# The start of each message-passing step of a graph layer: order of the first loads, place of one wait, and who clears the aggregation buffer

## The chip, the cores and the metric

The kernel runs on one core of a Trainium2 chip. The metric is the device time of one execution in microseconds (us), as the median of several runs. Engines are named as in the profile: PE (TensorE, with PEld for its weight loads), DVE (VectorE), ACT (ScalarE), POOL (GpSimd), SP (SyncE, which here only issues DMAs).

## The reference, cut to what matters

A graph layer over 3125 nodes with 256 channels and 50000 edges of three types. Three parts add up: gated graph convolution (below), a polynomial attention ("mix"), and an expert feed-forward part ("ffn").

```
def _gated_graph_conv(x, src, dst, emask, W, wih, whh, bih, bhh):
    h = x
    for i in range(STEPS):                    # 3 steps
        m = h @ W[i]
        msg = m[src] * emask[:, None]
        agg = segment_sum(msg, dst, num_segments=N)
        h = _gru_cell(agg, h, wih, whh, bih, bhh)
    return h
...
for t in range(T):                            # 3 edge types
    emask = (edge_type == t).astype(h.dtype)
    h_msg = h_msg + _gated_graph_conv(h, src, dst, emask, conv_w[t], gru_wih[t], ...)
```

## The kernel before

The program is a row of stages with a barrier between them: edge tables, normalisation, mix, the graph convolution (`gnn`, about 646 to 2457 us of the profiled execution), ffn. The change is inside `gnn`.

`gnn` does three steps (s = 0, 1, 2). The product with W[i] is moved behind the sum over edges, so a step first gathers rows of h and sums them by destination, and then multiplies by the product of the two weight matrices. A step has these parts:

- POOL gathers rows of h from a table in HBM (`tables[s]`: `xn_rows` in step 0, `h_rows` after), 128 edges at a time, by indirect DMA. Two gathers make a batch. One "pre" batch (line 1408) is followed by 195 main batches (line 1415), which fill a ring of 12 slots. So POOL issues 392 gathers in a step, one after another. The pre gather waits for an index tile (`pre_idx`) that DVE copies at line 1237; in steps 1 and 2 POOL waits before that for all stores of `h_rows`, which SP issues at line 1463.
- DVE makes a one-hot matrix for each batch (line 1238 for pre, 1260 for main), PE multiplies it with the gathered rows (line 1086, 8 matmuls a batch), and DVE adds the result to the right columns of `agg` (line 1245 for pre, 1257 for main). `agg` holds 6 x 3184 fp32 numbers in each partition and must be zero when the first batch is added. ACT clears it by eight activations (`act_clear`, line 1198), one for each group of nodes (NG = 8 groups of 224, 448 x 6 and 224 nodes); each adds one to the semaphore `cleared`.
- `pe_lead`: PE makes the weight products of type 0 (line 1114, 16 matmuls, which ACT copies to `g_wc`), the pre batch, the products of type 1, main batches 0 to 2, the products of type 2, and batches 3 to 8. The raw weights lie in buffers that hold node columns later: type 0 in `hn`, type 1 in `hT[1]`, type 2 in `hn` again. So the load of type 2 waits for the products of type 0.
- Then come 48 units (8 groups of nodes x 3 types x 2 halves of the channels) with the gates of the GRU cell (line 1163 on PE). Between their matmuls stand the other batches, at places written out beforehand by a planner (`PLAN`); before the first unit of group g, 24, 55, 87, 120, 152, 185, 195 batches must be in for g = 1 to 7. After the last gather lands, some 90 us of units are left in a step.

Every engine runs its instructions in the order in which they are written, so a wait holds up all that stands behind it. SP issues the loads of `gnn` in this order in step 0: node columns of group 0 (`load_states(0)`, three DMAs of 224 KB), the biases `bi` and `bh`, the three recurrent weights `wh` (768 KB each), then the raw weights (`load_weights`: 768 + 256 KB for each type).

In `dve_pre` the wait for `cleared` stands ahead of the copy of the indices:

```
step(e.tensor_copy(pre_at[:, :], bases[:, :]))
e.wait_ge(S["cleared"], NG * (s + 1))
...
e.tensor_copy(pre_idx[:, :], idx[...]).then_inc(V[s]["idx"], 1)
```

Of the kernel before, what the change touches and what calls it, by code (L numbers as in the profile page):

```python
# [10 lines left out]
ALU = mybir.AluOpType  # L11
# [5 lines left out]
P = 128  # L17
# [936 lines left out]
def halves_before(n):  # L954

    return sum(halves(i) for i in range(n))
# [36 lines left out]
def gnn(nc, A, tables, cols, idx0, idx1, keys, bases, main_at, shift, tab, iota_keys, ident, acc_rows, xf):  # L993

    with ExitStack() as ctx:
# [232 lines left out]
        def dve_pre(e, s):  # L1228
            rounds, number = pre_rounds(e)
            step = counted(e, V[s]["set"], 0)  # L1230
            step(e.memset(pre_shift[:, :], 0.0))
            step(e.tensor_copy(pre_at[:, :], bases[:, :]))
            e.wait_ge(S["cleared"], NG * (s + 1))
            idx = idx1 if s else idx0
            with e.Fori(0, rounds) as r:
                with e.Fori(0, number) as b:
                    e.tensor_copy(pre_idx[:, :], idx[:, bass.ds(b * BATCH + FIRST, BATCH)]).then_inc(V[s]["idx"], 1)  # L1237
                    e.scalar_tensor_tensor(out=onehot[:, 0, :, :], in0=iota_keys[:, :].unsqueeze(1).to_broadcast([P, BATCH, NKEY]), scalar=pre_shift[:, 0:1],
                                           in1=keys[:, bass.ds(b * BATCH, BATCH)].unsqueeze(2).to_broadcast([P, BATCH, NKEY]), op0=ALU.add, op1=ALU.is_equal).then_inc(V[s]["onehot"], 1)
                    e.tensor_copy(pre_now[:, :], pre_at[0:1, bass.ds(b, 1)]).then_inc(V[s]["now"], 1)  # L1240
                    e.wait_ge(V[s]["now"], r * NB + b + 1)
                    e.sem_inc(V[s]["seen"], 1)
                    o = e.value_load(pre_now[0:1, 0:1], min_val=0, max_val=NP)
                    e.wait_ge(V[s]["batch"], r * NB + b + 1)
                    e.tensor_tensor(agg[:, :, bass.ds(o, DT)], agg[:, :, bass.ds(o, DT)], pagg[0][:, :, :], ALU.add).then_inc(V[s]["added"], 1)
                    e.wait_ge(V[s]["added"], r * NB + b + 1)
                step = counted(e, V[s]["set"], r * 2 + 2)
                step(e.tensor_scalar(pre_shift[:, :], pre_shift[:, :], float(DT), None, ALU.add))
                step(e.tensor_scalar(pre_at[:, :], pre_at[:, :], DT, NP, ALU.add, ALU.min))  # L1249
            e.sem_inc(V[s]["done"], 1)  # L1250
# [144 lines left out]
        with nc.Block() as block:  # L1395
# [22 lines left out]
            def _(e):  # L1418
                def load_states(G):
# [6 lines left out]
                    for t in range(TYPES):  # L1426
# [1 line left out]
                        if s:  # L1428
                            e.wait_ge(col_store[t], 16 * ((s - 1) * NG + g + 1))
                        e.dma_start(hT[G % 2][:, t, :, 0:width(g)], src[:, :, node_at(g):node_at(g) + width(g)]).then_inc(h_in[G % 2], 16)  # L1430
                def load_weights(s):
                    for t in range(TYPES):
                        wi, wm = raw(t)
                        if s and t == 0:
                            for i in range(TYPES):
                                e.wait_ge(col_store[i], 16 * NG * s)
                            e.wait_ge(S["turn"], halves_before(TYPES * NG * s))
                        if s and t == 1:
                            e.wait_ge(S["pz"], s * UNITS)
                            e.wait_ge(S["d"], s * UNITS)  # L1440
                        if t == 2:
                            e.wait_ge(S["product"], 4 * TYPES * s + 4)
                        e.dma_start(wi, A["wihT"][t].rearrange("(k p) n -> p k n", p=P)).then_inc(w_type[t], 16)
                        e.dma_start(wm, A["convT"][t, s].rearrange("(k p) n -> p k n", p=P)).then_inc(w_type[t], 16)

                def load_base(g):
                    e.dma_start(base_of(g)[:, :, 0:width(g)], cols[0][:, :, node_at(g):node_at(g) + width(g)]).then_inc(base_in[g % 2], 16)
                load_states(0)
                e.dma_start(bi[:, :, :], A["bihT"]).then_inc(S["b_in"], 16)
                e.dma_start(bh[:, :, :], A["bhhT"]).then_inc(S["b_in"], 16)  # L1450
                for t in range(TYPES):
                    e.dma_start(wh[:, t, :, :], A["whhT"][t].rearrange("(k p) n -> p k n", p=P)).then_inc(S["w_in"], 16)
                load_weights(0)
                for G in range((STEPS - 1) * NG):
                    s, g = G // NG, G % NG
                    a, W = node_at(g), width(g)
                    load_states(G + 1)
                    for t in range(TYPES):
                        n = TYPES * G + t
                        e.wait_ge(S["hnew"], G * NU + KC * (t + 1))  # L1460
                        e.dma_start(cols[s + 1][t][:, :, a:a + W], hn[:, t, :, 0:W]).then_inc(col_store[t], 16)
                        e.wait_ge(S["rows_lo"], halves_before(n + 1))
                        e.dma_start(tables[s + 1][a + t * NP:a + t * NP + W, :].rearrange("(a p) c -> p a c", p=PT), rows16[n % 2][:, 0:W // PT, :]).then_inc(row_store[n % 2], 16)
                    if g == NG - 1:
                        load_weights(s + 1)
                s = STEPS - 1
                for v in range(UNITS + 6):
                    g = v // NU
# [36 lines left out]
            @block.scalar  # L1505
            def _(e):
                e.wait_ge(S["zero"], 1)
                for g in range(NG):
                    act_clear(e, 0, g)
                e.wait_ge(S["set"], 1)  # L1510
                for s in range(STEPS):
                    act_products(e, s)
                    for v in range(UNITS):
                        act_unit(e, s, v)
                        act_turn(e, s, v)
                        if last(s):
                            act_spreads(e, v)
                        if not last(s) and UNITS - NU <= v < UNITS - 1:
                            act_clear(e, s + 1, v - (UNITS - NU))
                    act_turn(e, s, UNITS)  # L1520
                    if last(s):
                        for v in range(UNITS, UNITS + 6):
                            act_spreads(e, v)
                    if not last(s):
                        for g in range(NU - 1, NG):
                            act_clear(e, s + 1, g)

            @block.vector
            def _(e):
                e.memset(zero[:, :], 0.0).then_inc(S["zero"], 1)  # L1530
                e.wait_ge(S["b_in"], 32)
                e.tensor_tensor(brz[:, :, :], bi[:, :, :], bh[:, :, :], ALU.add).then_inc(S["set"], 1)
                step = counted(e, S["rank"], 0)
                for s in range(STEPS):
                    dve_pre(e, s)
                    dve_batches(e, s, 0)
                    for v in range(UNITS + (6 if last(s) else 2)):
                        if v < UNITS:
# [390 lines left out]
```

## Time and profile before

| | |
|---|---|
| median of 3 runs | 3043.88 us (3043.86 to 3047.2) |
| the profiled execution, its own time | 3049.32 us |
| its span in the trace | 3047.6 us |
| PE busy | 2602.3 us (85%) |
| POOL busy | 1291.3 us (42%) |
| DVE busy | 1592.3 us (52%) |
| ACT busy | 651.8 us (21%) |
| mean granted TensorE clock | 0.927 of full speed |

Busy time is the sum of an engine's instructions, averaged over stages with different limits. Times in the trace count from the start of the span.

### The profile page before, as it was taken

The page shows a single profiled execution, that of the slowest core. Times are in us where ns is not written, and L with a number is a line of the kernel's source. Part 1 is how long each engine was busy: PE and PEld are TensorE (multiplying, and loading weights), DVE is VectorE, ACT ScalarE, POOL GpSimd, SP SyncE. Part 2 cuts the span into 40 slices and gives each one's busy share as a digit, 9 for nine tenths or more (in the row PEclk, how much of TensorE's full clock was granted, in tenths as well). Part 3 has the DMA queues.
Part 4 walks back from the last instruction along what each step waited for, and adds up shares of the span by engine and source line. Part 5 has one row for each costly group of instructions (what it writes and reads, how often), then busy time and mean ns, then how long its engine had stood idle before and what let it go on. Part 6 is the DMA issues. An engine that isn't in the chain of part 4 may idle for free. (4 is left out here: it accounts for less than half of the span.)

```text
span 3047.6 us, 39832 instructions
## 1 busy us (share of the span) xinstructions
PE 2602.3 (85%) x13041; PEld 1681.5 (55%) x13041; DVE 1592.3 (52%) x3093; ACT 651.8 (21%) x1191; POOL 1291.3 (42%) x1342
## 2 busy tenths in 40 slices
PE   1589899968999999889999997988988948999990
PEld 1343445536555555665555566555444647888880
DVE  4469887725555554465655544667777742000003
ACT  0321100031111112411111133122212312333320
POOL 0000000027777772377777705777777001111126
PEclk6699899989999999899999998999999957999995
DMA  1330076544454552544555425444444160222113
GB/s 50 104 106 1 1 266 231 203 138 133 140 157 145 157 157 83 155 144 133 152 159 156 148 90 158 133 130 141 140 139 134 34 197 24 64 92 90 62 50 115
DMA packets 211512, 374.19 MB, mean 123 GB/s; under 512 B 28898, under 2 KB 163459, under 8 KB 211206
## 3 DMA queue, kind: packets, MB, share of 16 engines
q1 hardware_dynamic: 149318, 203.45, 20.4%
q0 software_dynamic: 62016, 168.51, 19.3%
q8 instruction: 94, 1.54, 0.2%
q14 instruction: 84, 0.69, 0.1%
HBM read 299.54 MB, written 72.31 MB: 122 GB/s over the span
## 5 line engine op out<-in xcount | busy, mean ns | idle before, releaser
L1415 POOL DMA_INDIRECT g_ring<-h_rows,idx x780 | 771.6, 989 | 237.8 <-issue 207.0
L1086 PEld LDWEIGHTS g_pagg<-g_onehot,g_ring 128*128 128x128 f16 x4704 | 324.9, 98 | 404.7 <-issue 267.5
L1086 PE MATMUL g_pagg<-g_onehot,g_ring 128*128 128x144 f16 x4704 | 393.8, 228 | 139.7 <-DMA g_ring<-h_rows,idx 89.8
L1415 POOL DMA_INDIRECT g_ring<-xn_rows,idx x390 | 383.1, 982 | 118.9 <-issue 105.8
L1257 DVE TENSOR_TENSOR g_agg<-g_agg,g_pagg 128x288 f32 x585 | 265.7, 454 | 250.7 <-PE g_pagg L1086 207.8
L1260 DVE SCALAR_TENSOR_TENSOR g_onehot<-iota_keys,shift,keys 128x288 f16<-128x288 f16 x585 | 299.4, 513 | 1.0 <-DVE g_pre_at L1249 1.0
L1889 DVE TENSOR_TENSOR f_ys<-f_bank,f_b 128x256 f32<-128x256 f32 x58 | 24.6, 425 | 411.6 <-PE f_bank L1841 411.6
L1349 DVE SCALAR_TENSOR_TENSOR g_t<-g_ph,g_bh,g_rT 128x448 f32<-128x448 f32 (+1 forms) x144 | 90.0, 625 | 267.6 <-PE g_ph L1163 253.5
L1163 PE MATMUL g_pi<-g_agg,g_wc 128*128 128x448 f32 (+1 forms) x576 | 226.6, 517 | 0.0
L1163 PE MATMUL g_pr<-g_hT,g_wh 128*128 128x448 f32 (+1 forms) x576 | 223.9, 512 | 0.0
L1163 PE MATMUL g_pr<-g_agg,g_wc 128*128 128x448 f32 (+1 forms) x576 | 220.6, 506 | 0.0
L1163 PE MATMUL g_pz<-g_hT,g_wh 128*128 128x448 f32 (+1 forms) x576 | 219.7, 504 | 0.0
L1211 ACT ACTIVATE g_nT<-g_t,g_bi 128x448 f32<-128x448 f32 (+1 forms) x144 | 89.5, 622 | 607.8 <-DVE g_t L1356 607.8
L1163 PE MATMUL g_ph<-g_hT,g_wh 128*128 128x448 f32 (+1 forms) x576 | 218.8, 503 | 0.0
L1163 PE MATMUL g_pz<-g_agg,g_wc 128*128 128x448 f32 (+1 forms) x576 | 218.3, 501 | 0.0
L1841 PE MATMUL f_bank<-f_w,f_hid 128*128 128x256 f32 x928 | 207.9, 382 | 6.0 <-ACT f_hid L1864 6.0
L1833 PE MATMUL f_bank<-f_slotsT,f_w 128*128 x928 | 207.1, 382 | 1.0 <-ACT f_slotsT L1857 1.0
L1408 POOL DMA_INDIRECT g_ring<-xn_rows,g_pre_idx x2 | 2.1, 1044 | 472.1 <-DVE g_pre_idx L1237 471.8
L1841 PEld LDWEIGHTS f_bank<-f_w,f_hid 128*128 128x128 f32 x928 | 173.9, 190 | 35.2 <-issue 12.7
L1833 PEld LDWEIGHTS f_bank<-f_slotsT,f_w 128*128 128x128 f32 x928 | 177.7, 192 | 25.9 <-issue 1.4
L1777 POOL COPY f_now<-f_idx 128x2 int32 x30 | 5.5, 183 | 403.2 <-PE f_bank L1631 321.4
L1207 ACT ACTIVATE g_rT<-g_pr,g_brz 128x448 f32<-128x448 f32 (+1 forms) x144 | 84.5, 587 | 417.4 <-PE g_pr L1163 417.2
(345 smaller groups left out, 3465.5 us busy)
## 6 DMA issues: line engine op xcount, KB each, us to landing
ma_R<-q_cols SPq DMA_DIRECT2D x27, 896.0 KB, 9.8
f_w<-in_L_ffn_W SPq DMA_DIRECT2D x16, 1024.0 KB, 7.5
h_cols<-g_hn SPq DMA_DIRECT2D x36, 448.0 KB, 4.4
h_rows<-g_rows SPq DMA_DIRECT2D x36, 448.0 KB, 3.5
g_hT<-h_cols SPq DMA_DIRECT2D x36, 448.0 KB, 5.9
mix_R<-q_cols SPq DMA_DIRECT2D x15, 896.0 KB, 10.0
g_ring<-h_rows,idx POOLq DMA_INDIRECT x780
ma_R<-q_cols SPq DMA_DIRECT2D x9, 1120.0 KB, 5.6
```

The costliest lines, as they stand in the source:

```text
L1086: mm = e.matmul(pg[:, k * TYPES:(k + 1) * TYPES, :].rearrange("p t d -> p (t d)"), ring[:, slab, c, o:o + P], hot[:, c, :], start=(c == 0 ...
L1163: mm = e.matmul(p[:, 0:W], w, x, start=(first and k == 0), stop=(final and k == KC - 1), skip_group_check=True)
L1207: e.activation(rT[:, 0:W], pr[:, 0:W], ACT.Sigmoid, bias=brz[:, t, m:m + 1]).then_inc(S["r"], 1)
L1211: e.activation(nT[:, 0:W], t1[:, 0:W], ACT.Tanh, bias=bi[:, t, 4 + m:5 + m]).then_inc(S["n"], 1)
L1257: e.tensor_tensor(agg[:, :, bass.ds(o, DT)], agg[:, :, bass.ds(o, DT)], pagg[b % BANKS][:, :, :], ALU.add).then_inc(S["added"], 1)
L1260: e.scalar_tensor_tensor(out=onehot[:, b % 4, :, :], in0=iota_keys[:, :].unsqueeze(1).to_broadcast([P, BATCH, NKEY]), scalar=shift[:, 0:1] ...
L1349: e.scalar_tensor_tensor(out=t1[:, 0:W], in0=ph[:, 0:W], scalar=bh[:, t, 4 + m:5 + m], in1=rT[:, 0:W], op0=ALU.add, op1=ALU.mult).then_inc ...
L1415: e.indirect_dma_start(ring[:, b % SLABS, c, :], None, tables[s], bass.IndirectOffsetOnAxis(ap=idx[:, o:o + 1], axis=0)).then_inc(landed[b ...
L1777: e.tensor_copy(now[:, :], idx[:, bass.ds(t * 2, 2)]).then_inc(S["now"], 1)
L1833: mm = e.matmul(p1[m % 4], w1[:, x % 2, k, m * P:(m + 1) * P], slotsT[:, k, bass.ds(t * ST, ST)], start=(k == 0), stop=(k == KC - 1))
L1841: mm = e.matmul(p2[c], hid[:, m, c * P:(c + 1) * P], w2[:, x % 2, m, :], start=(m == 0), stop=(m == HC - 1))
L1889: e.tensor_tensor(ys[:, c, :], p2[c], b2[:, x, :], ALU.add).then_inc(S["result"], 1)
```

## The change

Four edits, all in `gnn`:

1. The wait for `cleared` in `dve_pre` moves from ahead of the index copy to ahead of the first addition into `agg`. This holds for all three steps.
2. In step 0 the clearing is divided: ACT clears groups 0, 2, 4, 6 and DVE groups 1, 3, 5, 7, by memset. In steps 1 and 2 ACT clears all groups, as before.
3. DVE's sum of the biases (`brz`) moves from ahead of `dve_pre` to behind it, and ACT waits for it (`set`) behind the weight products of step 0.
4. SP's loads in step 0 are put in the order: raw weights of type 0, biases, raw weights of type 1, node columns, recurrent weights, raw weights of type 2. `load_weights(s)` becomes `load_weight(s, t)` with the same waits.

```
 def dve_pre:
             step(e.tensor_copy(pre_at[:, :], bases[:, :]))
-            e.wait_ge(S["cleared"], NG * (s + 1))
...
                     o = e.value_load(pre_now[0:1, 0:1], min_val=0, max_val=NP)
+                    e.wait_ge(S["cleared"], NG * (s + 1))
                     e.wait_ge(V[s]["batch"], r * NB + b + 1)
                     e.tensor_tensor(agg[:, :, bass.ds(o, DT)], ...)
 SP:
-                load_states(0)
+                load_weight(0, 0)
                 e.dma_start(bi[:, :, :], A["bihT"]).then_inc(S["b_in"], 16)
                 e.dma_start(bh[:, :, :], A["bhhT"]).then_inc(S["b_in"], 16)
+                load_weight(0, 1)
+                load_states(0)
                 for t in range(TYPES):
                     e.dma_start(wh[:, t, :, :], ...).then_inc(S["w_in"], 16)
-                load_weights(0)
+                load_weight(0, 2)
 ACT:
                 e.wait_ge(S["zero"], 1)
-                for g in range(NG):
+                for g in range(0, NG, 2):
                     act_clear(e, 0, g)
-                e.wait_ge(S["set"], 1)
                 for s in range(STEPS):
                     act_products(e, s)
+                    if s == 0:
+                        e.wait_ge(S["set"], 1)
 DVE:
                 e.memset(zero[:, :], 0.0).then_inc(S["zero"], 1)
-                e.wait_ge(S["b_in"], 32)
-                e.tensor_tensor(brz[:, :, :], bi[:, :, :], bh[:, :, :], ALU.add).then_inc(S["set"], 1)
+                for g in range(1, NG, 2):
+                    a, n = node_at(g), width(g)
+                    e.memset(agg[:, :, a:a + n], 0.0).then_inc(S["cleared"], 1)
                 for s in range(STEPS):
                     dve_pre(e, s)
+                    if s == 0:
+                        e.wait_ge(S["b_in"], 32)
+                        e.tensor_tensor(brz[:, :, :], bi[:, :, :], bh[:, :, :], ALU.add).then_inc(S["set"], 1)
                     dve_batches(e, s, 0)
```

## Rows read from the trace of the kernel before

**Rows 1.** Busy time by stretch: stretch, length, PE, PEld, DVE, ACT, POOL, clock, DMA share, GB/s

```profile
641.00:693.00 52.00, 25.28 (x129) 15.79 (x129) 10.72 (x29) 23.94 (x21) 21.69 (x23) 0.75 0.63 209
693.00:1158.00 465.00, 429.56 (x2436) 262.37 (x2435) 273.97 (x573) 81.56 (x139) 354.97 (x362) 0.98 0.49 147
```

**Rows 2.** Costliest groups, POOL's gathers of steps 1 and 2

```profile
L1415 POOL DMA_INDIRECT g_ring<-h_rows,idx x780 | 771.6, 989 | 237.8 <-issue 207.0
```

**Rows 3.** What PE's batch matmuls (L1086) waited for: 1040:1110, 1160:1250, 1700:1750, 2350:2450

```profile
  DMA g_ring<-xn_rows,idx: 6.5, 8
...
  DMA g_ring<-xn_rows,idx: 2.0, 3
...
  DMA g_ring<-h_rows,idx: 3.8, 1
...
  DMA g_ring<-h_rows,idx: 1.9, 2
```

**Rows 4.** Timeline, start of step 0: start, length, engine, instruction, idle before and releaser

```profile
646.08 1.91 SPq L1430 DMA_DIRECT2D g_hT<-xn_cols  x3
646.15 0.06 DVE L1530 MEMSET g_zero<- 128x1 f32 x1 [4.24 <-PEq L88]
646.25 16.76 ACT L1198 ACTIVATE g_agg<-g_zero 128x1632 f32<-128x1632 f32 x8 [14.07 <-DVE g_zero L1530]
...
653.27 0.06 DVE L1231 MEMSET g_pre_shift<- 128x1 f32 x1 [1.42 <-issue]
653.37 0.25 DVE L1232 COPY g_pre_at<-bases 1x196 int32<-1x196 int32 x1
...
660.91 2.93 PE L1114 MATMUL g_pr<-g_hn 128*128 128x384 f32 x4 [19.73 <-DMA g_hn<-in_convT]
...
663.49 0.17 DVE L1237 COPY g_pre_idx<-idx 128x2 int32 x1 [9.88 <-ACT g_agg L1198]
...
664.60 1.14 POOL L1408 DMA_INDIRECT g_ring<-xn_rows,g_pre_idx  x1 [471.77 <-DVE g_pre_idx L1237]
```

**Rows 5.** Timeline, the last batch ahead of the first unit of step 0

```profile
692.10 1.12 PE L1086 MATMUL g_pagg<-g_onehot,g_ring 128*128 128x144 f16 x8 [1.80 <-DMA g_ring<-xn_rows,idx]
```

**Rows 6.** DVE's groups by shape, its fp32 memsets: busy, mean ns of one

```profile
L1871 DVE MEMSET f_none<- 128x256 f32 x1 | 0.3, 272 | 4.0 <-PEq L88 4.0
...
L1231 DVE MEMSET g_pre_shift<- 128x1 f32 x3 | 0.2, 59 | 2.8 <-issue 2.8
```

**Rows 7.** Timeline, start of step 1

```profile
1251.45 0.31 SPq L1463 DMA_DIRECT2D h_rows<-g_rows  x1
...
1252.21 0.25 DVE L1232 COPY g_pre_at<-bases 1x196 int32<-1x196 int32 x1
1252.37 0.50 SPq L1444 DMA_DIRECT2D g_hn<-in_convT  x1
...
1257.03 0.17 DVE L1237 COPY g_pre_idx<-idx 128x2 int32 x1 [4.57 <-ACT g_agg L1198]
...
1258.00 0.95 POOL L1408 DMA_INDIRECT g_ring<-h_rows,g_pre_idx  x1 [88.98 <-DVE g_pre_idx L1237]
1258.72 0.50 PEld L1114 LDWEIGHTS g_pr<-g_hn 128*128 128x128 f32 x2 [8.96 <-DMA g_hn<-in_convT]
...
1281.74 1.37 PE L1086 MATMUL g_pagg<-g_onehot,g_ring 128*128 128x144 f16 x16 [1.05 <-DMA g_ring<-h_rows,idx]
1284.75 1.12 PE L1086 MATMUL g_pagg<-g_onehot,g_ring 128*128 128x144 f16 x8 [1.64 <-DMA g_ring<-h_rows,idx]
```

**Rows 8.** The last store of `h_rows` ahead of steps 1 and 2, from issue to landing

```profile
DMA to landing us min/median/max: 2.4/2.4/2.4
...
DMA to landing us min/median/max: 2.8/2.8/2.8
```

**Rows 9.** Timeline, start of step 2

```profile
1842.58 0.31 SPq L1463 DMA_DIRECT2D h_rows<-g_rows  x1
...
1849.11 0.94 POOL L1408 DMA_INDIRECT g_ring<-h_rows,g_pre_idx  x1 [89.08 <-DVE g_pre_idx L1237]
```

More of the change, by code:

```diff
@@ L1430, in load_states, with load_weight @@
                         e.dma_start(hT[G % 2][:, t, :, 0:width(g)], src[:, :, node_at(g):node_at(g) + width(g)]).then_inc(h_in[G % 2], 16)
[L1431 to L1444, printed above, removed]
+                def load_weight(s, t):
+                    wi, wm = raw(t)
+                    if s and t == 0:
+                        for i in range(TYPES):
+                            e.wait_ge(col_store[i], 16 * NG * s)
+                        e.wait_ge(S["turn"], halves_before(TYPES * NG * s))
+                    if s and t == 1:
+                        e.wait_ge(S["pz"], s * UNITS)
+                        e.wait_ge(S["d"], s * UNITS)
+                    if t == 2:
+                        e.wait_ge(S["product"], 4 * TYPES * s + 4)
+                    e.dma_start(wi, A["wihT"][t].rearrange("(k p) n -> p k n", p=P)).then_inc(w_type[t], 16)
+                    e.dma_start(wm, A["convT"][t, s].rearrange("(k p) n -> p k n", p=P)).then_inc(w_type[t], 16)
@@ L1464, in _ @@
                     if g == NG - 1:
-                        load_weights(s + 1)
+                        for t in range(TYPES):
+                            load_weight(s + 1, t)
                 s = STEPS - 1
```

## Prediction

> **What bounds the kernel now.** The page calls PE busy for 85% of the span, but that is an average over stages, so I first read busy time by stretch. In the lead of step 0, 641 to 693 us, PE works 25.28 of 52 us at a mean clock of 0.75; in the 465 us behind it, 429.56 us at 0.98 [rows 1]. PE looks full there. Whether it is really the limit shows in what its batch matmuls wait for. They wait for a gather's landing in every part of a step, the last batches included: 6.5 us in eight waits late in step 0 and 2.0 us in three behind 1160 us, 3.8 us late in step 1, 1.9 us at the end of step 2 [rows 3]. In those moments PE has caught up with POOL. POOL itself waits for nothing but its own issue: 989 ns for a gather and (237.8 / 780 =) 0.30 us between two, the same gap at every one [rows 2]. 392 gathers take some 506 us, and the ring of 12 slots never holds POOL back.
>
> So a step is a clock that POOL starts with its first gather. From there to the last landing it runs freely; PE follows, now behind and now waiting, and behind the last landing come some 90 us of units that only PE sets. The next step starts when its rows are stored. The first gathers of the three steps start at 664.60, 1258.00 and 1849.11 [rows 4, 7, 9]. What the change is worth is how much earlier each of these comes, and PE's own start matters only if it is so late that the landing waits can't make it up. I then read the timeline around the three starts, for what releases the first gather.
>
> **Step 0, the clearing.** The first gather waits for the index copy (663.49), and this, for 9.88 us, for ACT's eight clearings, which end at 646.25 + 16.76 = 663.01 [rows 4]. The change takes this wait away and puts four memsets of DVE ahead of the index copy, so the question is how long those take. There is no large DVE memset in the trace. From the small ones: 59 ns at 1 element and 272 ns at 256 [rows 6], so (272 - 59) / 255 = 0.835 ns an element. Groups 1, 3 and 5 have 6 x 448 = 2688 elements in a partition, 2.30 us each; group 7 has 1344, 1.18 us: 8.1 us in all. DVE starts them at 646.21, ends at 654.3. Bounds: nothing in the rows is cheaper for an element; if DVE and ACT writing the same buffer at once slow each other to half speed, 16.2 us. I take 8.1, as the slope is from the same engine, operation and type.
>
> The Trainium skill ("VectorE: DVE Perf Modes", Zero memsets can be issued as uint32, and its clock of 0.96 GHz) says that a memset takes a cycle an element, 1.04 ns, whatever the type; by it the four would take an estimated 9.8 us, the sum below would be 11.5 instead of 13.2 us, and the time 3032.4. The trace differs, with 0.835 ns, and I go by the trace.
>
> Behind the memsets: DVE needs 1.42 us of issue before `pre_shift` (it loads the loop counts), as now; 0.35 us later `pre_at` is done [rows 4]: 656.1. Then the copy of the indices. Now it comes 0.48 us behind the release of its wait, and POOL's gather 1.11 us behind it (663.49 to 664.60) [rows 4]. So the copy starts at 656.6 and the gather at 657.7: **6.9 us earlier**. If the 1.42 us overlap with the memsets, up to 7.6 us. The moved `brz` addition ended at about 651.85 (1.42 ahead of 653.27); it now stands behind the pre batch, where DVE has 0.2 us to spare, and ACT needs it only in unit 0. ACT's four clearings take about half of 16.76 us, till some 654.8; `cleared` is asked for only by the addition of the pre batch, not before 662. Both cost nothing, covered by the wait for the gather.
>
> **Step 0, the loads.** PE starts its products at 660.91, after 19.73 us of waiting for the type 0 weights, which stand behind some 3 MB of other loads [rows 4]. Now they go out first. In step 1 the same pair starts PE 6.35 us behind the second of the two issues (1252.37 to 1258.72) [rows 7]; with SP starting at 646.08 and 0.7 us for the first issue that gives 653.2, 7.7 us earlier. This is not added to the gain: PE's work from the first product up to batch 7 was 22.0 us in step 1 (1258.72 to 1281.74, less 1.05 of waiting) [rows 7], so from 653.2 PE would be there by some 676 to 678 even with a wait for the pre gather. Batch 8, which POOL sets, comes now at 692.10, 27.5 us behind the first gather [rows 4, 5], then at 685.2. What the new order has past it: node columns and the recurrent weights are issued behind 2 MB of raw weights, but unit 0 (about 686) is the first to ask for them, and the whole 5.1 MB had landed by about 661 in the old order. The type 2 load still waits for the products of type 0; they start 7.7 us earlier and its use, which POOL sets, 6.9 us earlier, so it keeps its distance. All of edit 4 costs nothing and by itself gives nothing; without it (PE at 660.91) PE would reach batch 8 at about 684 to 686, so it covers edit 1 with little to spare.
>
> **Steps 1 and 2, the moved wait.** The clearings stay with ACT. The index copy waited 4.57 us for them in step 1 [rows 7] and about as much in step 2. Without that, the copy can go 0.48 us behind `pre_at` (1252.46), so at 1252.9, and the gather 0.97 us behind it at 1253.9. But something else is late next: POOL may not gather before the last `h_rows` store has landed, issued at 1251.45 and landing 2.4 us later, 1253.85 [rows 7, 8]. From there to the gather I take 0.8 us, which lay between the end of the index copy and the gather: 1254.65, so **3.35 us earlier**. In step 2: 1842.58 + 2.8 + 0.8 = 1846.2 against 1849.11 [rows 8, 9]: **2.9 us earlier**. If landing counts from the end of the issue, 0.3 less in each.
>
> PE's lead does not shift here, as the type 0 weights still land at 1258.7. It is then ready for batch 6 at 1280.69 and for batch 8 some 1.5 us later, at about 1282.3, where the old one came at 1284.75 [rows 7] and POOL alone would allow 1281.4. So unit 0 gains about 2.4 of the 3.35 us, and the rest comes at the next landing waits, which go on through the step [rows 3].
>
> A rule of the skill speaks against this edit: "DMA: Bandwidth & Descriptors" (Queues, rings and completion order) says that each DMA engine takes turns between the queues that have work for it, packet by packet. The earlier gathers would then be in among the weights for which PE waits. By rows: each gather is 128 KB, the two weight loads in flight are 2 MB and need 6.35 us; three gathers add at most 0.38 / 2 of that, 1.2 us. PE would then be for batch 8 at 1283.5, still ahead of 1284.75. It is a rival below.
>
> **The sum.** 6.9 + 3.35 + 2.9 = 13.2 us. The profiled execution's own time is 3049.32, so 3036.1 on its scale; that execution is 5.4 us above the median of 3043.88, and off the median I get **3030.7 us**, 0.43% less. Nothing else in the steps, in mix or in ffn is touched. All behind is carried forward by barriers.
>
> **Rivals.**
> - *PE becomes the bound in the leads of steps 1 and 2*, and does not catch up, because weights are delayed by the gathers and the catching up falls on batches where PE has no wait. Price: these steps give 1.2 to 2.4 instead of 3.35 and 2.9; in all 9.3 to 11.7, 3032 to 3034.5. For it: PE and landing are within 2 us of each other at 1281.74; against: waits for landings all along the step [rows 3]. Chance 0.15.
> - *Two engines that clear at once hinder each other.* If DVE needs 16.2 us, the copy comes at 664.7 and step 0 loses 1.2 instead of gaining 6.9; with steps 1 and 2 the gain is 5.1 us, 3038.8, within 0.2%. For it: nothing in the trace shows both engines writing one buffer at length. Against: nothing shows a loss either. Chance 0.06.
> - *The moved wait gives nothing in steps 1 and 2*, as the store lands later than it now seems (POOL's semaphore wait, or the weights beside it): only 6.9 us, 3037.0. Against: the landings of 2.4 and 2.8 us were measured with those weights in flight [rows 8]. Chance 0.05.
> - *Slower: POOL's pace suffers.* The whole time hangs on 1176 gathers at 1.29 us. A longer issue of each by 11 ns (13.2 / 1176) eats the gain, by 16 ns makes the kernel 0.2% slower. What could do it is the new position of the gathers against DVE's and SP's traffic: lengths already differ from 0.94 us [rows 9] to 1.14 [rows 4] with a mean of 0.989 [rows 2]. Against it: behind the lead everything PE, DVE and POOL do keeps its relative order. 3050 us and more. Chance 0.03.
>
> **How the numbers follow.** The forecast has a chance of 0.68; 0.03 is left for what I don't see, half of it a larger gain. A measurement of this kernel tells a difference from none at about 0.2%, 6.1 us, which is 3037.8. Faster: the forecast, the first rival, the third (barely), and most of the rest, 0.88. Same: the second and a part of the third, 0.09. Slower: 0.03. For the range: the bounds of the sum are 6.5 to 7.6, 3.0 to 3.4 and 2.6 to 2.9, so 12.1 to 13.9; the runs of before differ among themselves by 3.3 us, which can fall on either side; the low end is 3043.9 - 13.9 less 3.5, 3026.5, and the high end takes in the first rival and touches the third, 3037.
>
> **What the profile after should show.** Start of step 0: four DVE memsets of 2.3, 2.3, 2.3 and 1.2 us beside four ACT clearings; the index copy near 656.6 with no wait for ACT; the first gather near 657.7; PE's first product near 653; batch 8 near 685. In steps 1 and 2 the gap from the `h_rows` store's issue to the first gather falls from 6.5 us to 3.2 to 3.6. The length from a first gather to the end of its step stays as it is (664.60 to 1258.00, 593.4 us, falls only by the 3.35 of its end). The prediction is wrong if the memsets take over 3 us each, if the first gather of a step is not earlier, or if it is and the step's end is not: then PE, not POOL, set the steps.

## The result, and the profile after

| | before | after |
|---|---|---|
| median | 3045.67 us (8 runs, 3040.11 to 3047.2) | 3029.92 us (8 runs, 3024.84 to 3039.24) |
| profiled execution, own time | 3049.32 us | 3027.98 us |
| its span | 3047.6 us | 3026.3 us |

The ratio is 0.9953, 95% interval [0.994, 0.9966]: 14.3 us less, between 10.4 and 18.3. The forecast was 13.2 us less (3030.7 us). That the time meets the forecast within 0.8 us is in part luck: the forecast started from 3043.88 us, the median of three runs, and eight runs of the kernel before have 3045.67. So the start was 1.8 us too low, and this made up for most of the 2.6 us by which the medians moved more than forecast (15.75 against 13.2).

The start of step 0 in the timeline of the changed kernel, from SP's first load of the stage (here at 648.18, before at 646.08, as the part ahead of the stage took longer in this execution) to unit 0. Columns are start, length, engine, instruction, idle time before it and its releaser:

```profile
648.18 0.40 SPq L1442 DMA_DIRECT2D g_hn<-in_wihT  x1
648.35 8.56 ACT L1198 ACTIVATE g_agg<-g_zero 128x1632 f32<-128x1632 f32 x4 [14.06 <-DVE g_zero L1533]
648.85 2.30 DVE L1536 MEMSET g_agg<- 128x2688 f32 x1 [0.53 <-issue]
651.65 2.30 DVE L1536 MEMSET g_agg<- 128x2688 f32 x1 [0.51 <-issue]
653.66 2.93 PE L1114 MATMUL g_pr<-g_hn 128*128 128x384 f32 x4 [10.37 <-DMA g_hn<-in_convT]
654.46 2.30 DVE L1536 MEMSET g_agg<- 128x2688 f32 x1 [0.51 <-issue]
656.99 1.18 DVE L1536 MEMSET g_agg<- 128x1344 f32 x1 [0.23 <-issue]
658.12 0.06 DVE L1231 MEMSET g_pre_shift<- 128x1 f32 x1
658.89 0.17 DVE L1236 COPY g_pre_idx<-idx 128x2 int32 x1 [0.41 <-DVE g_pre_at L1232]
660.00 1.13 POOL L1408 DMA_INDIRECT g_ring<-xn_rows,g_pre_idx  x1 [465.61 <-DVE g_pre_idx L1236]
667.61 1.14 PE L1086 MATMUL g_pagg<-g_onehot,g_ring 128*128 128x144 f16 x8 [5.97 <-DMA g_ring<-xn_rows,g_pre_idx]
668.54 2.86 PE L1114 MATMUL g_pr<-g_hT 128*128 128x384 f32 x4
687.31 0.66 PE L1086 MATMUL g_pagg<-g_onehot,g_ring 128*128 128x144 f16 x8 [0.81 <-DVE g_agg L1257]
687.81 0.97 PE L1163 MATMUL g_pr<-g_hT,g_wh 128*128 128x224 f32 x4
```

The reader should see that the wait of the index copy is no longer for ACT, that the rows of the four memsets have 2.30 and 1.18 us with 0.51 or 0.23 us between them (what that means stands further down), and that the first gather comes 660.00 - 648.18 = 11.82 us into the stage where it came 18.52 before [rows 4].

The starts of steps 1 and 2 in the same timeline:

```profile
1242.96 0.31 SPq L1464 DMA_DIRECT2D h_rows<-g_rows  x1
1244.38 0.17 DVE L1236 COPY g_pre_idx<-idx 128x2 int32 x1 [0.41 <-DVE g_pre_at L1232]
1246.55 0.94 POOL L1408 DMA_INDIRECT g_ring<-h_rows,g_pre_idx  x1 [86.28 <-issue]
1250.32 2.93 PE L1114 MATMUL g_pr<-g_hn 128*128 128x384 f32 x4 [8.81 <-DMA g_hn<-in_convT]
...
1828.80 0.31 SPq L1464 DMA_DIRECT2D h_rows<-g_rows  x1
1832.36 0.94 POOL L1408 DMA_INDIRECT g_ring<-h_rows,g_pre_idx  x1 [85.14 <-issue]
```

The index copy is now done 2 us before POOL gathers, so it is no longer what POOL waits for. As the one that waited for the last store of `h_rows`, the profile names POOL's pre gather, in both steps. From the last row store's issue to the first gather it is 3.59 and 3.56 us, against 6.55 and 6.53 before [rows 7, 9].

With the same rows of every profile one execution can be cut in eight pieces: mix and all ahead of the stage; stage start to first gather; "body" of step 0 (first gather to the issue of the last `h_rows` store); gap; body 1; gap; body 2 (first gather to the first load of ffn, which stood at 2456.85 and stands at 2437.94 us); ffn. In us:

| | ahead | to first gather | body 0 | gap | body 1 | gap | body 2 | ffn |
|---|---|---|---|---|---|---|---|---|
| before | 646.1 | 18.52 | 586.85 | 6.55 | 584.58 | 6.53 | 607.74 | 590.8 |
| after | 648.2 | 11.82 | 582.96 | 3.59 | 582.25 | 3.56 | 605.58 | 588.4 |

The three pieces that the change touches give 6.70 + 2.96 + 2.97 = 12.6 us. The two profiled spans differ by 21.3, and the other 8.7 lie in pieces that nobody touched: bodies shorter by 8.4, ffn by 2.4, the part ahead longer by 2.1. The forecast had the length from the first gather of step 0 to that of step 1 fall from 593.4 us by 3.35; it fell by 6.8 (593.40 to 586.56 us). Is the rest the change too, or two executions that happened to differ? POOL's gathers in step 0 averaged 972 ns here. The experiments had to answer that.

### The profile page after: what moved, and what is told of

It reads as the page before. It is cut to its first block and busy times, and to the rows that moved or that the text cites. A ratio compares the mean times of both kernels' runs of the same rounds, so it can differ in the third digit from the quotient of the medians.

```text
span 3026.3 us, 39832 instructions
## 1 busy us (share of the span) xinstructions
PE 2598.2 (86%) x13041; PEld 1679.7 (56%) x13041; DVE 1599.0 (53%) x3097; ACT 642.7 (21%) x1187; POOL 1277.8 (42%) x1342
## 5 line engine op out<-in xcount | busy, mean ns | idle before, releaser
L1086 PEld LDWEIGHTS g_pagg<-g_onehot,g_ring 128*128 128x128 f16 x4704 | 324.4, 98 | 395.0 <-issue 252.1
L1086 PE MATMUL g_pagg<-g_onehot,g_ring 128*128 128x144 f16 x4704 | 391.5, 227 | 133.1 <-DMA g_ring<-h_rows,idx 78.3
L1415 POOL DMA_INDIRECT g_ring<-xn_rows,idx x390 | 379.1, 972 | 118.8 <-issue 103.9
```

The source lines that it names most:

```text
L1086: mm = e.matmul(pg[:, k * TYPES:(k + 1) * TYPES, :].rearrange("p t d -> p (t d)"), ring[:, slab, c, o:o + P], hot[:, c, :], start=(c == 0 ...
L1415: e.indirect_dma_start(ring[:, b % SLABS, c, :], None, tables[s], bass.IndirectOffsetOnAxis(ap=idx[:, o:o + 1], axis=0)).then_inc(landed[b ...
```

## The experiments

Theory A is that of the prediction: a body is POOL's run of 392 gathers and a fixed tail, so the time moves by what the first gathers move. Rival B: PE's lead sets the steps. Rival C: earlier gathers make the bodies shorter.

**Edit 1 alone** (the moved wait on the kernel before).

```
-            e.wait_ge(S["cleared"], NG * (s + 1))      # ahead of the index copy
...
+                    e.wait_ge(S["cleared"], NG * (s + 1))  # ahead of the addition
```

> Edit 1 alone on the kernel before: the wait for the clearing moves behind the index copy in all steps; ACT clears all, loads in the old order. Theory A (the first gather of each step sets the time, PE catches up): in step 0 the index copy comes right behind the bias addition, first gather about 9 us behind the stage's first load issue instead of 18.5, so 9.5 us earlier, and 3.0 us earlier in each of steps 1 and 2: 15.5 us less than before, the same as the full change. Rival B (PE's lead sets it): PE's products still start 14.8 us into the stage, batch 8 comes 7 us earlier in step 0 and 2.4 to 3 in the others: 12 us less. In both, the gap from the last row store to the first gather is 3.6 us instead of 6.5 in steps 1 and 2.

Measured: 3027.18 us against 3044.11, ratio 0.9941 [0.9929, 0.9954], 18.0 us less. The first gather came 8.70 us into the stage, unit 0 at 42.8 us, 3.1 later than in the changed kernel at 39.6. The time is not later. One of four edits gives the whole gain, within what these runs can tell.

**Edit 1 undone.**

```
+            e.wait_ge(S["cleared"], NG * (s + 1))
...
-                    e.wait_ge(S["cleared"], NG * (s + 1))
```

> The changed kernel with edit 1 undone: the wait for the clearing stands ahead of the index copy again, the clearing shared and the new order of loads kept. Theory A: step 0 keeps its 6.7 us, as DVE's own memsets end last; steps 1 and 2 fall back to a gap of 6.5 us from row store to first gather. 6.7 us less than before, 6 us more than the changed kernel. Rival C (the steps' bodies get shorter because gathers start earlier, which the profile of the changed kernel seemed to show with 8 us beyond the sum): then this kernel loses some 6 + 5 us against the changed one, and the length from first gather to last row store goes back from 582.5 to 585 in steps 0 and 1.

Measured: 3036.91 us, ratio 0.9975 [0.9966, 0.9984], 7.6 us less than before. To first gather 11.81, gaps 6.55 and 6.53, bodies 0 and 1 584.57 and 583.80. So step 0 keeps its 6.7, the gaps return, and the bodies lie between those of the first two profiles. Rival C had them return to 585, and 6.7 us separate this kernel from the changed one in the two ratios where theory A has 6 and rival C some 11, with intervals of 3 and 4 us to either side. This run alone doesn't end rival C; the next one does.

**Edit 2 undone**: ACT clears all eight groups in step 0.

```
-                for g in range(0, NG, 2):
+                for g in range(NG):
                     act_clear(e, 0, g)
...
-                for g in range(1, NG, 2):
-                    a, n = node_at(g), width(g)
-                    e.memset(agg[:, :, a:a + n], 0.0).then_inc(S["cleared"], 1)
```

> The changed kernel with edit 2 undone: ACT clears all eight groups in step 0, DVE none, so DVE copies the indices at once. Theory A: first gather about 4 us behind the stage's first load issue instead of 11.8: 7.8 us less than the changed kernel, 20.5 less than before. Rival B: ACT is busy clearing till 17 us into the stage, so its copies of the weight products, and PE behind them, come late; PE reaches batch 8 only 2 us earlier than in the changed kernel or no earlier, and the time is that of the changed kernel within 2 us.

Measured: 3022.73 us, ratio 0.9929 [0.9916, 0.9942], 21.6 us less than before. Its timeline in step 0:

```profile
647.37 0.40 SPq L1442 DMA_DIRECT2D g_hn<-in_wihT  x1
647.54 16.76 ACT L1198 ACTIVATE g_agg<-g_zero 128x1632 f32<-128x1632 f32 x8 [14.06 <-DVE g_zero L1533]
649.01 0.06 DVE L1231 MEMSET g_pre_shift<- 128x1 f32 x1 [1.50 <-issue]
650.87 1.13 POOL L1408 DMA_INDIRECT g_ring<-xn_rows,g_pre_idx  x1 [456.93 <-DVE g_pre_idx L1236]
653.14 2.93 PE L1114 MATMUL g_pr<-g_hn 128*128 128x384 f32 x4 [10.66 <-DMA g_hn<-in_convT]
664.44 0.46 DVE L1245 TENSOR_TENSOR g_agg<-g_agg,g_pagg 128x288 f32 x1 [13.97 <-ACT g_agg L1198]
664.82 2.90 PE L1114 MATMUL g_pr<-g_hT 128*128 128x384 f32 x4 [3.42 <-ACT g_wc L1121]
683.06 0.97 PE L1163 MATMUL g_pr<-g_hT,g_wh 128*128 128x224 f32 x4
```

What rival B named is there: DVE's first addition waits for ACT's clearing, and PE waits for ACT. Yet the first gather is 3.50 us into the stage, and the time follows the gather. Bodies 0 and 1 are 585.13 and 585.12 us, so gathers that start 8.3 us earlier than in the changed kernel did not make them shorter: rival C is out. Sharing the clearing works against the change, since DVE clears ahead of the index copy.

**Edit 4 undone**: the old order of loads.

```
-                load_weight(0, 0)
+                load_states(0)
                 # biases
-                load_weight(0, 1)
-                load_states(0)
                 # recurrent weights
-                load_weight(0, 2)
+                for t in range(TYPES):
+                    load_weight(0, t)
```

> The changed kernel with edit 4 undone: loads of step 0 in the old order, so PE's first product comes 14.8 us into the stage instead of 5.5. Theory A: the first gather stays where it is and PE makes up for it: same time as the changed kernel within 1 us. Rival B: PE needs 22 us of own work up to batch 8, which then comes some 39 us into the stage, where the changed kernel has it at 39.1: also near nothing at the unit, up to 2 us lost; so a loss over 3 us would speak against both and for the weights' order as the source of the gain.

Measured: 3028.94 us, ratio 0.9955 [0.9942, 0.9968]. Unit 0 came 39.4 us into the stage, in the changed kernel 39.6. The new order is worth nothing here. PE's first product came 15.82 us into the stage instead of 5.48, the pre batch 23.46 instead of 19.43, and from there to unit 0 PE's rows show a single wait of 0.20 us, while in the changed kernel it waited among its batches and ran its first products behind the pre batch at the lower clock (below).

**Edits 1 and 3 alone** (both undoings together).

> Edits 1 and 3 alone: moved wait, and the bias addition behind the pre batch; ACT clears all groups in step 0 and the loads stand in the old order. Theory A: first gather 3.5 us into the stage, as where only edit 2 was undone; PE's first product is back at 14.8 us and unit 0 comes some 3 to 6 us later than there (about 40 instead of 35.7 us into the stage), and PE makes it up before the step ends: the time is that of the kernel with edit 2 undone within 2 us, 20 us less than before. Rival B: what unit 0 loses stays lost, 4 us more than with edit 2 undone.

Measured: 3027.81 us against 3046.47, ratio 0.9937 [0.9924, 0.9951], 19.2 us less. Its timeline:

```profile
645.06 1.91 SPq L1430 DMA_DIRECT2D g_hT<-xn_cols  x3
648.58 1.13 POOL L1408 DMA_INDIRECT g_ring<-xn_rows,g_pre_idx  x1 [456.41 <-DVE g_pre_idx L1236]
665.85 2.93 PE L1114 MATMUL g_pr<-g_hn 128*128 128x384 f32 x4 [25.68 <-DMA g_hn<-in_convT]
688.55 0.97 PE L1163 MATMUL g_pr<-g_hT,g_wh 128*128 128x224 f32 x4
```

Here PE is at unit 0 only 39.97 us behind the first gather; with edit 2 undone it was 32.19, in the changed kernel 27.81. The bodies of step 0 are 585.89, 585.13 and 582.96 us. So PE made up 7.0 of 7.8 us between the first two; the third had the quicker gathers (972 against 980 ns). PE catches up, as theory A says. It is these lengths that say so and not the time: theory A asked for the time of edit 2 undone within 2 us, rival B for 4 us more, and 19.2 against 21.6 us less lies between them. Two things came otherwise than expected: unit 0 is 7.8 us later into the stage than with edit 2 undone, not 3 to 6, and beside edit 1 alone the first gather is 5.2 us earlier (edit 3's part) where the measured gain grew by 1.2 us, which intervals of 4 us to either side can't tell from 5. PE's first product is 20.8 us into the stage instead of 14.8 [rows 4], as early gathers now go out ahead of the weights.

**All clearing on DVE.**

```
-                for g in range(0, NG, 2):
-                    act_clear(e, 0, g)
...
-                for g in range(1, NG, 2):
-                    a, n = node_at(g), width(g)
+                for g in range(NG):
+                    a, n = node_at(g), width(g) + (DT if g == 0 else 0)
```

> The changed kernel with all eight groups of step 0 cleared by DVE, ahead of the index copy. This leaves PE's loads alone and delays only the first gather: six memsets of 2.3 us, 1.4 and 1.2, with about 0.5 between them, 10.3 us more than in the changed kernel, so the first gather at 22.1 us into the stage. Theory A: the whole time goes up by 10.3 us against the changed kernel, one for one. If PE set the step, less than half of it.

Measured: first gather 21.95 us into the stage, 10.13 more than in the changed kernel. 3045.68 us against 3046.47, ratio 0.9999 [0.9989, 1.0009]. The pieces ask for 2.5 us less than before (-3.43 + 2.95 + 2.96); the result is 0.3 less, from 3.4 less to 2.7 more. Beside the changed kernel it is 14.0 us more by the two ratios, with intervals of 4 and 3 us to either side; theory A asks for 10.1 and a step set by PE for less than half of that. PE's loads were those of the changed kernel; the gain went with the gather.

**A memset on POOL for each batch of step 0**, first of one element, then of 256.

```
+                        if s == 0:
+                            e.memset(pool_extra[:, b:b + 1], 0.0)
                         for c in range(BATCH):     # two gathers
```

> The changed kernel with one added POOL memset of 128x1 ahead of each of the 195 main batches of step 0, into a buffer that nobody reads. It puts 0.1 us of work and between 0 and 0.3 us of issue on POOL each time, 20 to 78 us in all. Theory A, that POOL's pace sets the length from first gather to last row store: this length grows by just what POOL's gathers take longer, read from POOL's own rows, and steps 1 and 2 stay as they are. If PE set the steps, the growth would be smaller by what slack PE's landing waits leave: none, as more waits only add up; so a growth of less than 15 us would end theory A.

Measured: 3035.86 us, ratio 0.9966 [0.9952, 0.9979], body 0 585.21 us, 2.25 more than in the changed kernel. By the letter of the expectation, a growth under 15 us ends theory A. But it took for granted that POOL's row would grow, and this hardly did: gathers, idle time and memsets are 501.5 us (381.8 + 96.6 + 23.1) against 497.9, and 2.7 us of that are slower gathers. The dose was next to none, so the run decides nothing. The rows of POOL in this run:

```profile
701.31 0.95 POOL L1418 DMA_INDIRECT g_ring<-xn_rows,idx  x1 [0.30 <-issue]
702.26 0.11 POOL L1415 MEMSET g_pool_extra<- 128x1 f32 x1
702.56 0.94 POOL L1418 DMA_INDIRECT g_ring<-xn_rows,idx  x1 [0.19 <-issue]
```

702.56 - 701.31 is 1.25 us, the pace of two gathers with nothing between them (their starts are 1.25 us apart elsewhere too): the memset fits in the 0.30 us gap. So it was made 0.33 us long.

> As the run with the added POOL memset, which put no time on POOL's row because 0.12 us fitted into the gap between two gathers, but with a memset of 128x256, some 0.3 us, ahead of each of the 195 batches of step 0. That should take each pair of gathers from 2.5 to about 2.7 to 2.8 us, 39 to 58 us over the step. Theory A: the length from the first gather to the last row store of step 0 grows by what POOL's row grows, within 2 us, and the two other bodies stay. If PE had been setting the step (as its 92% busy share suggests), 465 us with 37 us of PE idle would let part of it vanish: a growth of 25 us or less.

This run fell on a chip on which the kernel before takes 3339.0 us. Measured: 3329.35, ratio 0.9972 [0.9963, 0.9982], body 0 longer by 3.5 us (683.36 against 679.86 for the changed kernel there). The expectation was 39 to 58 us; on that chip POOL is held back by full slots (below), so the run says nothing on the ordinary ones. The same kernel again:

> The added 0.33 us POOL memset ahead of each batch of step 0 once more. The first time the run fell on a chip on which the kernel before takes 3339 us and POOL is held back by the ring (PE sets the steps there), so the dose vanished in POOL's waiting: the first body grew by 3.5 us only. If this run falls on a chip like those of the first profiles (before near 3045 us), theory A says: POOL's run of gathers in step 0 grows by 195 times some 0.2 us, 35 to 50 us, and the body of step 0 and the whole time by the same within 2 us, steps 1 and 2 as before. A growth below 25 us would say that PE sets the steps there too. On a chip near 3339 us: again 3 to 6 us.

This time the kernel before took 3046.58 us. Measured: 3070.75 us, ratio 1.0085 [1.0068, 1.0102]. POOL's groups, added work last:

```profile
L1420 POOL DMA_INDIRECT g_ring<-xn_rows,idx x390 | 382.2, 980 | 90.9 <-issue 61.8 <-POOL g_pool_extra L1417 29.0
L1417 POOL MEMSET g_pool_extra<- 128x256 f32 x195 | 64.3, 330 | 0.1
```

POOL's row in step 0 is now 382.2 + 90.9 + 64.4 = 537.5 us, in the changed kernel 497.9 (below): 39.6 more. Body 0 went from 582.96 to 620.45, 37.5 more; bodies 1 and 2 are 582.85 and 608.83. The expectation had 35 to 50 us, body like row within 2. Though PE is 92% busy there [rows 1], what POOL loses the step loses.

**Two repeats.** The kernel before, for a second profile:

> The kernel before, unchanged, for a second profile. The profile of the changed kernel had bodies of the steps (first gather to last row store) shorter by 3.9 and 2.3 us than the one of before, with a mean gather of 972 against 982 ns in step 0. If that is the spread between executions, this profile shows a first body between 582 and 587 us that goes with its mean gather by 392 times the difference; if it belongs to the change, it is again above 586.

The time was 3046.27 us (one run), body 0 585.28 us with gathers of 981 ns: 1.6 us shorter than in the first profile of the same kernel. And the changed kernel beside the one with edit 2 undone:

> The changed kernel again, for a second profile and to stand beside the next run on the same chip. If the short bodies of its first profile were the spread between executions, the first body lies anywhere between 582 and 587 us and goes with the mean gather of step 0.

> The changed kernel with edit 2 undone, again, on the same chip as the changed kernel. Theory A: its first gather starts 8.3 us earlier in the stage; of this 6 to 8 us remain in the time.

These two ran on the chip of 3339.0 us: 3323.59 us, ratio 0.9957 [0.9943, 0.997], and 3319.69, ratio 0.9936 [0.9922, 0.9949]. The second body-0 measurement of the changed kernel can't be set beside the first, 679.86 against 582.96 us. The expected 6 to 8 us between the two kernels came as 3.9. The intervals of the ratios overlap, but all five runs with edit 2 undone (at most 3320.80 us) lie below all five of the changed kernel (at least 3320.94).

## Why the prediction was right

The mechanism held: the first gather of each step sets the time. Some terms of the sum were mis-sized, and it is luck that the errors nearly cancel. One reading was too strong: "POOL itself waits for nothing but its own issue" rests on a row that has 207.0 of 237.8 us as issue [rows 2]. For the rest the profile names PE's batch matmuls. It does no harm, since no single one of these gaps is longer than 0.3 us, the gap that POOL has anyway.

**The first term, 6.9 us, measured 6.70.** The rows of the memsets have 2.30 and 1.18 us, as worked out from 0.835 ns an element. But that is not what the memsets cost. From one start to the next it is 2.80 and 2.81 us (648.85, 651.65, 654.46), and in the run where DVE clears all groups 2.80 or 2.81 for each pair of 2688. The idle time ahead of a memset goes with the size of the memset behind it: 0.51 us ahead of 2688 elements, 0.23 ahead of 1344, both with ACT clearing beside it and without. Duration and gap together are 2.81 / 2688 = 1.045 and 1.41 / 1344 = 1.049 ns an element. A fixed start-up of each memset doesn't fit that, but a row whose end is right and whose start is too late does. Either way a memset costs more than its row says. The Trainium skill ("VectorE: DVE Perf Modes", Zero memsets can be issued as uint32) has a cycle an element, and with its clock of 0.96 GHz an estimated 2.8 us for 2688 elements. The trace agrees, 2.80 and 2.81 us from start to start; the prediction set this rate aside for the 0.835 ns of the rows, and that was the wrong reading.

From the end of the `zero` memset (648.31) to the end of the last one (658.17) it is 9.86 us, where the sum had 8.1. The 1.42 us of issue that it had behind them vanished: `pre_shift` starts at 658.12, at once, while it has 1.50 us of issue ahead of it in the kernel where DVE clears nothing. 8.1 + 1.42 = 9.5 against 9.86: two wrong terms, one nearly right sum. The rival of two engines hindering each other fell: ACT's four took 8.56 us, about half of its former 16.76, and DVE's pace is the same with and without ACT.

**The second, 3.35 and 2.9 us, measured 2.96 and 2.97.** The step "something else is late next" holds: POOL's gather now comes 2 us behind the index copy, and 3.6 us behind the store. From landing to gather the sum had 0.8 us. It is 1.2: in the runs where the store's landing is on record the gap is 3.56 to 3.62 us at a landing of 2.4, and 3.86 in the one case with 2.7 (step 2 of edits 1 and 3). In step 1 this made the gain 0.4 us less than the 3.35 forecast. In step 2 the forecast had a landing of 2.8 us, and the gap after fits one of 2.4, so two errors cancel. PE's lead cost less than the forecast had it: unit 0 of step 1 stands 31.48 us behind the last store's issue instead of 34.22, 2.7 us earlier of 2.96.

**That PE makes up what it lacks** is shown by the body lengths of edit 1 alone and of edits 1 and 3 alone, and that POOL's clock is the one that counts by the all-DVE clearing and by the longer memset. The table puts the pieces of each profile beside the measured times, in us less than before. Each sum is (18.52 - first) + (6.55 - gap) + (6.53 - gap); each measured value is (1 - ratio) times the median of before in that comparison.

| | first gather | gaps | sum | measured, interval |
|---|---|---|---|---|
| changed kernel | 11.82 | 3.59, 3.56 | 12.6 | 14.3, 10.4 to 18.3 |
| edit 1 alone | 8.70 | 3.57, 3.56 | 15.8 | 18.0, 14.0 to 21.6 |
| edit 1 undone | 11.81 | 6.55, 6.53 | 6.7 | 7.6, 4.9 to 10.3 |
| edit 2 undone | 3.50 | 3.58, 3.62 | 20.9 | 21.6, 17.7 to 25.6 |
| edit 4 undone | 11.82 | 3.59, 3.57 | 12.6 | 13.7, 9.7 to 17.7 |
| edits 1 and 3 | 3.52 | 3.57, 3.86 | 20.7 | 19.2, 14.9 to 23.2 |
| DVE clears all | 21.95 | 3.60, 3.57 | 2.5 | 0.3, -2.7 to 3.4 |
| memset of one element | 11.82 | 3.60, 3.59 | 12.6 | 10.4, 6.4 to 14.6 |

All eight sums lie in their intervals. The memset of 256 elements makes a ninth: 12.6 less the 39.6 us that POOL's row grew is 27.0 us more than before, and 25.9 more were measured (20.7 to 31.1). With intervals of 3 to 5 us to either side the table can't place a difference of 3 us; the two runs that moved POOL by 10 and by 40 us carry it. Rival B would have put edit 1 alone 3 us behind the changed kernel.

**The 8.7 us that belong to no edit** are the spread between executions: the first body goes with the mean gather, and the kernels that share an edit don't share a body. Mean gather of step 0 and body 0, over the profiles on ordinary chips: 972 ns and 582.96 us (changed), 972 and 582.04 (edit 4 undone), 975 and 583.81 (edit 1 alone), 978 and 584.57 (edit 1 undone), 979 and 585.20 (DVE clears all), 980 and 585.13 (edit 2 undone), 980 and 585.89 (edits 1 and 3), 981 and 585.28 (before again), 982 and 586.85 (before). Ten nanoseconds times 392 gathers are 3.9 us. Two of the groups:

```profile
L1415 POOL DMA_INDIRECT g_ring<-xn_rows,idx x390 | 379.1, 972 | 118.8 <-issue 103.9 <-PE g_pagg L1086 14.9
```

for the changed kernel, and for the kernel before, second profile:

```profile
L1415 POOL DMA_INDIRECT g_ring<-xn_rows,idx x390 | 382.6, 981 | 118.9 <-issue 105.5 <-PE g_pagg L1086 13.4
```

From the last gather's start to the row store it is 82.3 to 83.6 us in all of these. Kernels with the same edits in steps 1 and 2 had body 1 anywhere from 581.75 to 585.52. Why a gather's mean differs from run to run is open, and so is whether an order of work could make it smaller.

**Where a step was wrong.** "PE would be there by some 676 to 678" for batch 7 in step 0: it came in the batches of 685. The sum had left out that the pre gather, now among the loads, lands late: PE counts the pre batch 7.6 us behind the first gather (660.00 to 667.61), having idled 5.97 us; before, it was 4.6 us (664.60 to 669.20). Behind this idling the granted clock was at 0.50, its 1.2 GHz level, for the next products, which took 2.86 us for four:

```profile
658.00:667.00 9.00, 3.64 (x10) 1.67 (x8) 1.12 (x6) 1.47 (x3) 5.48 (x6) 0.88 1.00 353
668.50:671.50 3.00, 3.00 (x8) 1.79 (x6) 1.63 (x6) 0.06 (x1) 2.09 (x4) 0.50 0.46 134
```

(busy time by stretch, columns as in [rows 1]; the DMA share is 1.00 while PE waits). The batches then waited for DVE's one-hots, and batch 8 came 27.3 us behind the first gather, as it had at 27.5. PE's lead of some 7 us in the sum was in truth none. It cost nothing, since PE catches up anyway.

"Without it PE would reach batch 8 at about 684 to 686" was the cover that edit 4 was to give. Edit 4 undone had unit 0 at the same place, so the cover was not needed.

**Version that beats both.** The changed kernel with edit 2 undone: 21.6 us less than the kernel before, where the changed one has 14.3. On the other chip it was 3.9 us below the changed one in the same comparison. Its first gather is 8.3 us earlier in the profile; that it is faster than the changed kernel is likely, as all runs of one lie below all of the other there, though the intervals of the ratios overlap in both comparisons.

## What to carry to other kernels

When an engine is 92% busy and yet waits now and then, all along, for the same producer, the producer's start and pace set the time; look for what stands ahead of its first instruction. Of several edits that "start earlier", only those on the producer's own path count, and here one moved wait gave all. Before sharing a job between engines, look at what is queued behind it: the memsets cost 8.3 us of start, because the index copy stood behind them. And take the cost of an instruction from start to start of its neighbours before trusting its own duration: here the row had 2.30 us of 2.80.

The rule on the producer is one for the state it was seen in. On the slower chip below, POOL waits for PE, and the same reading would mislead.

## What was not expected of the hardware

- **Gathers and loads share the way in, and the earlier one wins.** With the old order of loads and gathers from 3.5 us into the stage, PE's weights allowed the first product at 20.8 us instead of 14.8. The four kernels with the old order line up: first gather at 18.52, 11.82, 8.70 and 3.52 us into the stage, first product at 14.84, 15.82, 19.37 and 20.79. With the weights issued first, the same early gathers left it at 5.8 us (653.14 - 647.37), and the changed kernel has 5.5. The rule cited from the Trainium skill ("DMA: Bandwidth & Descriptors", Queues, rings and completion order), that a DMA engine takes turns between queues, agrees in direction. In steps 1 and 2 the feared 1.2 us did not show: from store to first product it is 7.07 to 7.42 us in step 1 with early gathers and 7.15 to 7.27 without, in step 2 7.33 to 7.60 and 6.91 to 7.39.
- **An fp32 memset on DVE costs more than its row says:** 0.835 ns an element in the row, 1.05 from start to start (above).
- **A POOL memset of 0.12 us between two gathers costs next to no time,** one of 0.33 us costs about 0.2.
- **A chip 10% slower on this kernel.** There the ratio of the changed kernel was the same (0.9957), but the steps were set otherwise. POOL's group in the changed kernel there:

```profile
L1415 POOL DMA_INDIRECT g_ring<-xn_rows,idx x390 | 383.9, 984 | 195.2 <-issue 101.6 <-remote 58.7 <-PE g_pagg L1086 34.8
```

and what the batch matmuls of PE waited for, over the whole run, there and then on an ordinary chip (the first lines of each list):

```profile
  issue: 762.9, 1240
  DMA g_ring<-xn_rows,g_pre_idx: 12.2, 2
```

```profile
  issue: 252.1, 591
  DVE g_onehot L1260: 141.1, 198
  DMA g_ring<-h_rows,idx: 78.3, 84
```

  A gather takes as long as elsewhere (984 ns), but POOL's idle time is 195.2 instead of 118.8 us, with single waits of up to 4.7 us. In the program POOL waits there for a free slot only, so PE is the one behind. That fits with the 0.33 us memset all but vanishing. The list of what PE waited for can't say more: the profiles of that chip have no landing of any main gather on record, so a wait for one would stand under "issue" as well. But some of PE's idle time there falls inside a group of four matmuls, ahead of which the program waits and within which it doesn't. From the changed kernel with edit 2 undone, on that chip:

```profile
716.43 0.82 PE L1163 MATMUL g_pr<-g_agg,g_wc 128*128 128x224 f32 x3 [0.36 <-issue]
717.85 0.35 PE L1163 MATMUL g_ph<-g_hT,g_wh 128*128 128x224 f32 x1 [0.59 <-issue]
718.58 0.48 PE L1163 MATMUL g_ph<-g_hT,g_wh 128*128 128x224 f32 x1 [0.38 <-issue]
719.30 1.10 PE L1163 MATMUL g_ph<-g_hT,g_wh 128*128 128x224 f32 x2 [0.25 <-issue]
```

  In step 0 of the changed kernel there are 17 such stops there, 6.7 us, and none on the ordinary chip, where a group of four runs through in 0.92 us. They are a small part of PE's idle time, and what causes them and the rest is open. That the gain was the same there is not explained by theory A. There is no profile of the kernel before on that chip, so what the change did to PE's start on it isn't known; with edit 2 undone unit 0 came 52.3 us into the stage and in the changed kernel 64.4, with bodies of 679.80 and 679.86 us.
